# Three first loads issued by ScalarE, another order in head and groups, and silu's table loaded right behind each exp

## What is computed

```python
xn = _layernorm(x, axis=-1)
q = jnp.einsum('bse,edh->bsdh', xn, Wq) + bq        # k, v alike, 8 heads repeated to 32
scores = jnp.einsum('bsdh,bseh->bsde', q, k) / sqrt(16)
s = jnp.einsum('bsde,bseh->bsdh', softmax(scores), v)
nx = xn * rsqrt(mean(xn**2) + 1e-5) * ln_w
f = (silu(nx @ gate_w.T) * (nx @ up_w.T)) @ down_w.T
x = x + s * silu(f)
```

## Time and profile before

| | |
|---|---|
| three timed runs | 487.92, 489.51 and 489.67 us, median 489.51 |
| the profiled execution | 488.14 us |
| its span | 486.4 us |
| TensorE clock granted, mean | 0.999 of full speed |
| TensorE's matmuls busy | 473.5 us, 97% |
| VectorE busy | 395.4 us, 81% |
| ScalarE busy | 227.1 us, 47% |
| GpSimd busy | 119.4 us, 25% |
| DMA, mean | 216 GB/s |

### The profile page before, as it was taken

One profiled execution on the slowest core, in us unless ns is written; L12 is line 12 of the kernel. 1 busy time (PEld: TensorE's weight loads), 2 busy tenths in 40 slices (PEclk: granted clock), 3 DMA queues, 4 the chain that ended last, 5 costly groups with the idle time before them and its releaser, 6 DMA issues.

```text
span 486.4 us, 6166 instructions
## 1 busy us (share of the span) xinstructions
PE 473.5 (97%) x2148; PEld 394.6 (81%) x2148; DVE 395.4 (81%) x539; ACT 227.1 (47%) x378; POOL 119.4 (25%) x106
## 2 busy tenths in 40 slices
PE   7999999999999999999999999999999999999996
PEld 7888888888888888879898787878878888878884
DVE  6779679789989888739996889988898889996704
ACT  5784665686686664383114132432432432447101
POOL 5820212222212342243232101111111111127900
PEclk9999999999999999999999999999999999999999
DMA  8806689767675764683262659555655555513762
GB/s 269 326 1 235 258 299 393 259 248 263 252 259 211 285 241 194 216 325 122 95 205 98 225 200 350 197 195 216 218 194 218 216 194 195 194 44 129 272 247 87
DMA packets 27326, 105.12 MB, mean 216 GB/s; under 512 B 2848, under 2 KB 4128, under 8 KB 23968
## 3 DMA queue, kind: packets, MB, share of 16 engines
q1 hardware_dynamic: 27296, 104.74, 58.9%
HBM read 68.29 MB, written 36.44 MB: 215 GB/s over the span
## 4 chain that ended last, share of the span: by engine, by line
PE 77%; DVE 11%; ACT 5%; issue 4%; DMA 1%; SPq 0%; POOL 0%; ACTq 0%; DVEq 0%
PE gu_ps L502 15%; PE gu_ps L505 15%; PE gu_ps L504 15%; PE y_ps L643 7%; PE y_ps L645 7%; PE y_ps L644 7%; PE gu_ps L644 3%; PE gu_ps L643 3%; PE gu_ps L645 3%; DVE prod L1170 1%; PE gu_ps L665 1%; PE gu_ps L666 1%; PE gu_ps L669 1%; DVE attn L1173 1%; DVE z_lo L1076 1%
## 5 line engine op out<-in xcount | busy, mean ns | idle before, releaser
L502 PE MATMUL gu_ps<-z_hi,w_ops 128*128 128x512 f32 x364 | 142.4, 391 | 3.6 <-ACT gu_ps L831 3.6
L505 PE MATMUL gu_ps<-z_hi,w_ops 128*128 128x512 f32 x364 | 141.7, 389 | 0.0
L504 PE MATMUL gu_ps<-z_lo,w_ops 128*128 128x512 f32 x364 | 141.7, 389 | 0.0
L447 POOL TENSOR_TENSOR h_lo<-h,h_hi 128x512 fp32r<-128x512 f32 x28 | 38.9, 1389 | 226.3 <-ACT h_hi L868 226.3
L502 PEld LDWEIGHTS gu_ps<-z_hi,w_ops 128*128 128x128 f32 x364 | 68.3, 188 | 20.8 <-issue 6.5
L505 PEld LDWEIGHTS gu_ps<-z_hi,w_ops 128*128 128x128 f32 x364 | 68.3, 188 | 14.3
L504 PEld LDWEIGHTS gu_ps<-z_lo,w_ops 128*128 128x128 f32 x364 | 68.4, 188 | 13.8
L643 PE MATMUL y_ps<-wd_ops,h_hi 128*128 128x512 f32 x168 | 65.7, 391 | 0.2 <-POOL h_lo L447 0.2
L645 PE MATMUL y_ps<-wd_ops,h_lo 128*128 128x512 f32 x168 | 65.6, 390 | 0.0
L644 PE MATMUL y_ps<-wd_ops,h_hi 128*128 128x512 f32 x168 | 65.5, 390 | 0.0
L868 ACT ACTIVATE h_hi<-h 128x512 fp32r<-128x512 f32 x28 | 17.7, 632 | 91.1 <-DVE h L1128 91.1
(11 more groups left out here) (131 smaller groups left out, 761.5 us busy)
## 6 DMA issues: line engine op xcount, KB each, us to landing
w_kept<-w_ops SPq DMA_DIRECT2D x13, 1792.0 KB, 5.7
w_ops<-w_kept SPq DMA_DIRECT2D x13, 1792.0 KB, 7.4
wd_ops<-wd_kept SPq DMA_DIRECT2D x35, 512.0 KB, 4.1
raw<-gate_up SPq DMA_DIRECT2D x28, 256.0 KB, 3.1
wd_kept<-wd_ops SPq DMA_DIRECT2D x14, 512.0 KB, 7.2
xz<-x SPq DMA_DIRECT2D x16, 256.0 KB, 5.3
raw<-down SPq DMA_DIRECT2D x14, 256.0 KB, 7.3
w_ops<-wd_kept SPq DMA_DIRECT2D x7, 512.0 KB, 7.8
```

Of the source, the lines that this page charges most:

```text
L447: pool.tensor_tensor(lo, src, hi.bitcast(F32), ALU.subtract).then_inc(h_lo_done, 1)
L502: pe.matmul(acc, w_h, z_hi[:, zi, c, :], start=start and c == 0, stop=False, skip_group_check=True)
L504: pe.matmul(acc, w_h, z_lo[:, zi, c, :], start=False, stop=False, skip_group_check=True)
L505: end = pe.matmul(acc, w_l, z_hi[:, zi, c, :], start=False, stop=c == 1, skip_group_check=True)
```

## The change

Five things change; TensorE's and GpSimd's instructions and their order don't.

1. ScalarE issues the loads of x tiles 1 and 3 and of gate weights 0, ahead of its first table load; SP issues tiles 0 and 2 and goes on with ln_w and Wq.
2. Weights of slice 0: first_hi multiplies by ln_w and rounds in one instruction of 128 columns (four for gate, four for up), where scale and hi_a took five. first_lo makes the low half on VectorE in four instructions that multiply and subtract, where lo_a took one.
3. Order in the head. VectorE: both halves of wqkv_lo stand behind tile 4's statistics, times_up0(0) moves back behind two z_lo tiles. ScalarE: z_tile(7), z_hi(7) and wd and h_hi of slice 0 change places, and group 1's seed goes ahead of t_hi(0, 3).
4. exps ends with load_silu, an activation of one column that has silu's table loaded there. Between the pairs the first of the two exps goes behind the h_hi of item 24.
5. The steps of attention in the second pair: 116 in the table where there were 130; the other 14 stand behind group 27, 6 ahead of finish(2, 0) and 2 behind each of the finish(2, j). By the new table exps stand in groups 18, 21, 24 and 27, where they stood in 17, 20, 23 and 26.

```diff
-                       ((0, 3, 4, 0), (0, 7, 3, 1), (0, 5, 3, 0), (0, 6, 2, 0), (1, 6, 2, 1), (0, 5, 3, 0),
-                        (0, 6, 2, 0), (1, 6, 2, 1), (0, 5, 3, 0), (0, 7, 2, 1), (1, 5, 4, 0), (1, 5, 3, 1),
-                        (0, 6, 4, 0), (2, 6, 3, 1)))
+                       ((0, 0, 5, 0), (0, 5, 4, 0), (0, 5, 2, 0), (0, 4, 2, 0), (1, 6, 1, 1), (1, 6, 3, 0),
+                        (1, 4, 2, 0), (1, 6, 1, 1), (0, 6, 3, 0), (1, 5, 2, 0), (1, 6, 3, 1), (0, 4, 3, 0),
+                        (1, 5, 2, 0), (1, 6, 3, 1)))
...
-            load_x(0, range(0, J))
+            load_x(0, range(0, J, 2))
             sp.dma_start(lnw_sb[:], lnw).then_inc(lnw_in, 16)
-            load_gate(0)
...
+            def first_hi(part):
+                act.wait_ge((gate_in, up_in)[part][0], 16)
+                for m, c, k in first_places(part):
+                    end = act.activation(w_ops[:, 0, 0, m, c * P:(c + 1) * P], gu_raw[:, 0, 2 * m + c, :], ACT.Copy,
+                                         scale=lnw_sb[:, k:k + 1])
+                end.then_inc(w_hi_a, 1)
...
+            def load_silu():
+                silu_loads[0] += 1
+                act.wait_ge(table_loaded, silu_loads[0])
+                act.activation(scratch[:, 1:2], scratch[:, 0:1], ACT.Silu).then_inc(table_loaded, 1)
...
+                if pairs:
+                    load_silu()
...
+            act.dma_start(xz[:, 1, :], x_tiles[1]).then_inc(x_in[1], 16)
+            act.dma_start(xz[:, 3, :], x_tiles[3]).then_inc(x_in[3], 16)
+            act.dma_start(gu_raw[:, 0, 0:K, :], gate_up[0, :, 0:E].rearrange("p (c n) -> p c n", n=P))\
+               .then_inc(gate_in[0], 16)
+            load_silu()
...
+                if u == 2 * NI - 4:
+                    exps(exps_in(NI)[:1])
+            exps(exps_in(NI)[1:])
...
+            def first_lo(part):
+                dve.wait_ge(w_hi_a, part + 1)
+                for m, c, k in first_places(part):
+                    t = slice(c * P, (c + 1) * P)
+                    end = dve.scalar_tensor_tensor(w_ops[:, 0, 1, m, t], gu_raw[:, 0, 2 * m + c, :], lnw_sb[:, k:k + 1],
+                                                   w_ops[:, 0, 0, m, t].bitcast(F32), ALU.mult, ALU.subtract)
+                end.then_inc(w_lo_a, 1)
...
-            attention(STEPS)
+            attention(6)
             for j in range(J):
                 finish(2, j)
+                attention(2)
+            attention(STEPS)
```

## The result

The changed kernel took 483.02 us (median of 4 executions, 482.99 to 483.06) and the kernel before, beside it, 489.35 us (487.92 to 489.67, 4 executions). The ratio is 0.9876 with a 95% interval of 0.9857 to 0.9896: 1.2% faster. The profiled execution took 483.06 us with a span of 481.2, where the one before had 486.4.

The account below looks back on a forecast made before the run. TensorE, busy 97% of the span, was taken as the bound, so only its waits count: 2.8 (head) + 0.7 + 0.8 + 1.65 - 1.1 = 4.85 us gained from 488.8, giving 484.0 us, range 481.5 to 487.3.

Parts of the forecast that it names:

- The loads: Head, up to the first real matmul: split loads and no separate rounding gain 0.3 us, bounds 0.6 gained and 1.1 lost.
- wqkv_lo: Head: its second half moves ahead of tile 5's statistics on VectorE, so the whole 0.5 us wait is gained.
- The last z_lo: Head: its z_hi copy no longer stands behind h_hi and wd of slice 0; 1.1 us gained.
- the first seed: Group 1: the seed no longer stands behind t_hi, needing only m1 and silu1; 1.2 us gained.
- VectorE's full stretch: VectorE, busy 15.90 of 16 us between 30 and 46 us, may not keep up; 0.3 us taken off the head's gain.
- The pair change: Between the pairs: the first exp three h_hi earlier gains 0.7 us at group 14's h0; fewer steps gain 0.8 in group 15.
- The later seeds: Groups 16 to 26: silu's table loaded right behind exp while ScalarE would idle removes the remaining seed waits; 1.65 us gained.
- The last group: Group 27: exp and its loads ahead of item 41's h_hi add a wait; 1.1 us lost (0.8 or 1.7 depending on GpSimd).
- (a): Rival: tiles 0 and 2 come late and VectorE passes it on, nothing left of the head's 2.8; 486.8 us, chance 0.17.
- (b): Rival: second half gives nothing, VectorE late in some group and the last group's wait 1.7; 486.0 us, chance 0.13.
- (c): Rival: a table load costs more than its row, delaying seeds and the last group's h_hi; 489.2 us, chance 0.05.
- (d): Rival: steps moved to the tail slow GpSimd's low halves above 2.7 us each, starving TensorE; 491.5 us, chance 0.05.

Follow-up runs that it names:

- e4: Changed kernel with the attention steps and tail put back as before (130 steps in the second pair's table, exps in groups 17, 20, 23, 26): 482.95 us.
- e9: Changed kernel with the rounding of slice 0's down weights moved from behind the last copies to between z_tile(4) and z_tile(5): 482.51 us.
- e12: Changed kernel with group 27's exp behind item 41's h_hi, slice 0's down weights copied earlier, one attention step moved to group 17, seven more transposes: 480.90 us.
- e13: e8 with ten more transposes of the constant between the transposes of tile 3 and the first real matmul: 482.01 us.
- e8: Changed kernel with slice 0's weights made as before (scalings in place, one rounding of 512 columns, one instruction for the low half): 483.47 us.
- e10: Changed kernel with both the attention steps put back as before and the early silu table load left out: 485.60 us.
- e3: Changed kernel without the small silu activation behind each exp, so silu's table is loaded in front of the next silu: 482.94 us.
- e6: Changed kernel with two more table loads (exp's, then silu's, each with a small activation) behind each exp: 497.73 us.

## Why the prediction was right, and where it was not

**The sum.** 484.0 us was forecast, 483.02 measured. A gain of 4.85 was forecast, and 5.13 were gained by TensorE's matmuls between the profiled executions; that the sum is so near is partly luck, since terms missed by -0.3, -0.8, +0.7 and +0.2 and cancelled. The rest of the difference of 1.0 is the start. The sum was taken from 488.8, the middle of four executions, where the one whose trace was read took 488.14; from that, 5.13 less is 483.01. The kernel before varies by 1.7 us between executions, and no run explains why.

**The loads (0.3 forecast, 0.02 measured).** Two chains end at the first real matmul. The prediction weighed how late the tiles could land, and took the gate weights to land as before. In the kernel before the gate weights set it, 4.04 us ahead; tile 3 would have allowed 11.05 (9.00 and 2.05), so without the rounding 0.40 were to be had. With the split tile 3 is normalised 0.38 later, and the gate weights are scaled 0.63 later (8.04 for 7.41), which uses up nearly all of the 0.68 that the rounding gave on that side. The mark that it set (11.1) was missed; 11.7, from which the step would have been wrong in sign, wasn't reached in this execution, but in e4, e9 and e12, with the same loads, it was (12.81, 12.41 and 11.88).

**wqkv_lo (0.5 forecast, -0.27 measured).** This step failed. At wqkv_lo itself only 0.2 are gained, 0.2 are lost ahead of it behind the first low half, and 0.27 behind it at the transposes of tiles 4 and 6. The step counted what moved out from ahead of wqkv_lo, a microsecond of statistics, and not what stood ahead of both: the second low half in four pieces, priced at 0.3 us more and taking 1.28 more than e13's one piece (1.97 for 0.69), 0.85 more than e8's. e13 shows it by undoing it. The price had been set for the first low half, where it was 0.45 (1.13 for 0.68); the second runs beside GpSimd's additions.

**The last z_lo, the first seed, VectorE's full stretch.** 1.1, 1.2 and -0.3 were forecast; 1.20, 1.24 and -0.34 came. For the first two the waits stood in the trace before with their releasers and are gone at just these matmuls (26.09 and 43.78 above), but no run takes these moves back, so they are read from the two traces and not shown by an experiment. take_u2, for which it counted under 0.1 us to spare, is a little late: m7 of group 1 loses 0.09, which stands in the row of groups 2 to 13. For the allowance the prediction named no instruction; the trace names t_add beside wd_lo and h_lo on GpSimd, which came together because the change put wd ahead of h_hi behind the copies. e9 takes it away. m6 of group 1 was to start near 43.9 and starts at 44.95: 1.0 of the head's 2.8 are missing, in the two steps told first.

**The pair change (0.7 and 0.8).** Right in size, 0.81 and 0.81. In cause: e10 leaves the first and takes the second, as the prediction had it, but the empty place ahead of h0 of group 14 that it named as well isn't needed.

**The later seeds (1.65 forecast, 2.39 measured).** The size failed at the list of waits. It shows idle time only, and a seed can be late by up to 0.16 us plus the slower pace of two matmuls without any: records overlap. In the kernel before, the seed of group 21, behind the exp of group 20:

```profile
356.07 0.39 PE L505 MATMUL gu_ps<-z_hi,w_ops 128*128 128x512 f32 x1
356.49 0.47 PE L502 MATMUL gu_ps<-z_hi,w_ops 128*128 128x512 f32 x1
356.80 0.40 PE L504 MATMUL gu_ps<-z_lo,w_ops 128*128 128x512 f32 x1
```

The distance is 0.42 and then 0.31 where it should be 0.23 twice, and no wait is noted. There and behind the exp of group 23 the change gained 0.32 and 0.23, and behind each visible wait 0.08 more than the 0.16 counted. The cause was half right. The prediction gave all of it to the early load, and thought of the new table only as a thing that does no harm. Either gives nearly all (e3, e4, e10), so the early load, added last, is worth 0.4 us behind the exps of groups 18, 21 and 24 and 0.3 behind those of 5 and 8, and costs 0.9 in the last group: by itself it is worth nothing here.

**The last group (-1.1, measured -0.87).** The chain was right link by link: exp, loads, h_hi, GpSimd, TensorE. GpSimd took 1.28 us instead of the 1.5 taken; the 0.8 named for that case was nearer.

**The rivals.** (a) The head gave 1.85, between the forecast's 2.8 and the rival's nothing. (b) The second half gave 3.1, and the seeds behind the exps are on time, though groups 19, 22 and 24 have more steps than before; group 16's seed still waits 0.37 for c12 of group 15. (c) A table load costs its row: at 430.25 + 1.28 exp starts 0.01 later, and the room of 2.0 us was 2.1 in e6. That holds for the second half; in groups 5 and 8 it was 0.4, and two more loads were too many there. The Trainium skill ("ScalarE: Activation LUTs", "What ACT_TABLE_LOAD costs") counts 1.38 us of drain with a load; no trace here shows any. (d) GpSimd's low halves took 1.70 us each in the tail (22.08 by 13) where it would have had to be 2.7, and VectorE ended 9 us early. (The prediction's 13 x 0.6 is 7.8 and not 7.5, so its rival stood at 491.8. And the lower end of its range, 481.5, is 0.7 below what it is said to come from: 487.92 less 4.85 and 0.9 is 482.2.)

## What to carry to other kernels

Compare the start of the same instruction on the bounding engine in two traces; the steps of that difference find gains of 0.1 us that a list of idle times leaves out. When two things stand ahead of a late instruction, take each back alone and both together before giving either the credit: here, at the seeds behind the exps of the second pair, each was worth 0.4 us or less with the other there, and 1.9 to 2.3 with the other gone. Cutting an instruction in four for a fused multiplication has to be priced beside what runs there: 0.45 us undisturbed, 1.28 here; and everything behind it in the engine's order pays, not only the reader of its result. Where two chains end at one instruction, measure both: taking 0.68 us out of one gave nothing once the loads had moved both.

## What the runs showed of the hardware

TensorE's clock fell from 2.4 to 1.2 GHz for seven to nine matmuls behind pauses of 1.32, 1.90, 2.29, 2.40 and 3.6 us, and did not behind others of 1.2 and of 2.29: the length of the pause alone doesn't decide. Each fall cost about 0.2 us a matmul, 1.3 to 1.6 us in all. In the head it turned a gate load that landed 1.0 us late into 2.4 us at the eighth matmul.

VectorE instructions with both inputs in SBUF are stretched by GpSimd here; the reduces, with one input, aren't. In the tail, beside the low halves on GpSimd, the products of two tensors took 2.34 and 2.20 us where 1.23 is their time alone, and the reduces between them 1.22:

```profile
437.62 2.34 DVE L1200 TENSOR_TENSOR prod<-scores,qkv 128x1024 f32<-128x1024 f32 x1
440.00 1.22 DVE L1203 TENSOR_REDUCE attn<-prod 128x64 f32<-128x1024 f32 x1
```

The Trainium skill ("SBUF — State Buffer", "Who interferes with whom") states this as a rule, and the trace agrees. Which of the two is stretched goes by which starts first: in e13 VectorE's 0.69 us instruction kept its time and GpSimd's took 1.04 for 0.64, and in e8, started 0.09 us behind GpSimd's, VectorE's took 1.12.
